# Layer 2's selective scan: the drive of eight states scaled on a turned du and turned back by TensorE

## The reference

```python
x_dbl = jnp.einsum('bkdl,kcd->bkcl', xs, x_proj_w)
dts_r, Bs, Cs = (x_dbl[:, :, :R], x_dbl[:, :, R:R + N], x_dbl[:, :, R + N:])
dts = jnp.einsum('bkrl,kdr->bkdl', dts_r, dt_proj_w)
dt = jax.nn.softplus(dts + dt_proj_b[None, :, :, None])
...
def step(h, inp):
    dt_l, u_l, B_l, C_l = inp
    dA = jnp.exp(dt_l[..., None] * A)
    h = h * dA + (dt_l * u_l)[..., None] * B_l[:, :, None, :]
    y = jnp.einsum('bkdn,bkn->bkd', h, C_l)
    return (h, y)
...
ys = ys + Ds.reshape(1, K, d, 1) * xs
```

## Time and profile before

| | before |
|---|---|
| median of three runs | 42401.93 us |
| profiled execution, its own time | 42416.64 us |
| its span, first to last instruction | 42414.8 us |
| mean granted clock of TensorE in it | 0.866 of full speed |
| busy over the span: DVE, POOL, PE, ACT | 82%, 73%, 71%, 48% |

### The profile page before, as it was taken

The page is one execution under the profiler, slowest core; times in us unless marked ns, Lnnn a source line. Parts: engine busy times, 40 slices in busy tenths (PEclk is TensorE's granted clock), DMA queues, the critical chain, the costliest instruction groups (busy, mean ns, idle before and its releaser), DMA issues. The chain is left out here.

```text
span 42414.8 us, 275743 instructions
## 1 busy us (share of the span) xinstructions
PE 30144.3 (71%) x63524; PEld 11806.2 (28%) x63524; DVE 34737.8 (82%) x35406; ACT 20384.3 (48%) x37797; POOL 31168.8 (73%) x14520
## 2 busy tenths in 40 slices
PE   6767767777777777777767777777777777777777
PEld 3232232322323223232232322323223232232322
DVE  7959779597795977959779597795977959779597
ACT  4535445354453544535445354453544535445354
POOL 6939769397693976939769397693976939769397
PEclk8888888888888888888888888888888888888888
DMA  3414234142241422414234142341423414234142
GB/s 105 151 37 152 84 105 152 37 152 85 103 152 36 152 84 104 152 36 152 84 105 151 38 152 84 105 151 37 152 84 105 151 37 152 84 105 151 37 152 84
DMA packets 1221654, 4486.01 MB, mean 106 GB/s; under 512 B 144528, under 2 KB 146072, under 8 KB 1211680
## 3 DMA queue, kind: packets, MB, share of 16 engines
q1 hardware_dynamic: 1219872, 4466.97, 30.4%
HBM read 4399.30 MB, written 67.11 MB: 105 GB/s over the span
## 5 line engine op out<-in xcount | busy, mean ns | idle before, releaser
L567 PE MATMUL PS<-WORK,CST 128*128 128x512 f32 x36096 | 20046.6, 699 | 8354.6 <-POOL WORK L483 7561.8
L472 POOL TENSOR_TENSOR WORK<-WORK,XN 128x1024 f32<-128x1024 f32 x8192 | 19246.1, 2381 | 1.3
L567 PEld LDWEIGHTS PS<-WORK,CST 128*128 128x128 f32 x36096 | 7593.5, 222 | 20499.9 <-POOL WORK L483 10379.6
L921 ACT ACTIVATE PS<-WORK,AN 128x512 f32<-128x512 f32 x16384 | 10604.8, 678 | 1806.7 <-DVE WORK L1446 1092.8
L1438 DVE TENSOR_TENSOR_SCAN PS<-PS,HST,WORK 128x512 f32<-128x512 f32 x8960 | 10972.5, 1271 | 45.5 <-ACT PS L921 32.1
L1438 DVE TENSOR_TENSOR_SCAN WORK<-PS,HST,WORK 128x512 f32<-128x512 f32 x5376 | 6583.7, 1267 | 0.0
L483 POOL TENSOR_TENSOR WORK<-WORK,CWIDE 128x1024 f32<-128x1024 f32 x2048 | 4859.8, 2373 | 136.2 <-issue 83.0
L530 POOL MEMSET XN<- 128x66 f32 x32 | 4.9, 153 | 5777.4 <-DVE SM L1288 5675.4
L921 ACT ACTIVATE WORK<-PS 128x512 f32<-128x512 f32 (+3 forms) x2752 | 1628.6, 598 | 5296.8 <-PE PS L567 4589.4
L1446 DVE TENSOR_TENSOR WORK<-PS,WORK 128x1024 f32<-128x1024 f32 x3072 | 3762.3, 1225 | 105.1
L921 ACT ACTIVATE HST<-PS 128x2 f32<-128x2 f32 x4480 | 748.9, 167 | 6154.6 <-DVE WORK L1446 6154.0
(11 more groups left out here) (158 smaller groups left out, 27665.1 us busy)
## 6 DMA issues: line engine op xcount, KB each, us to landing
XN<-xbc_rows SPq DMA_DIRECT2D x4096, 512.0 KB, 3.7
WORK<-xbc_rows SPq DMA_DIRECT2D x2048, 512.0 KB, 3.9
CWIDE<-xbc_rows SPq DMA_DIRECT2D x2048, 512.0 KB, 4.2
BIG<-in_spec_dram SPq DMA_DIRECT2D x32, 2048.0 KB, 14.7
X<-in_x_dram SPq DMA_DIRECT2D x16, 2048.0 KB, 8.7
xbc_rows<-WORK SPq DMA_DIRECT2D x512, 64.0 KB, 3.2
out_dram<-X SPq DMA_DIRECT2D x16, 2048.0 KB, 6.3
TAP<-in_cw_dram SPq DMA_DIRECT2D x1, 576.0 KB
```

The source lines that it names most:

```text
L472: nc.gpsimd.tensor_tensor(S.both(S.Q[u % 6]), S.both(S.DU[u // SN % 2]), S.wide(S.BW, u).unsqueeze(1).to_broadcast([P, 2, NT]), MUL).then_ ...
L567: return nc.tensor.matmul(o, w, r, start=start, stop=stop)
L921: return nc.scalar.activation(o, i, f, **k)
```

## The change

1. **Turned states.** For the eight states of `TURNED_STATES` POOL no longer makes the drive. Once per group, PE turns `DU` (eight transposes of 128 x 128, `turn_du`) and the rows of B (`turn_b`), and ACT copies both to SBUF (`copy_dut`, `copy_bt`). With positions on the partitions, the row B of a state is one value per partition, so ACT's `scale` makes the drive by four scaled copies of 256 columns into the single buffer `ST`. PE's `turn_back` (eight transposes) puts it, channels on the partitions again, into the pair of PSUM banks of the unit. The decay of such a unit goes to `Q` in SBUF, and the scan reads the drive from PSUM.
2. **Who weighs.** `POOL_STATES` grows from six to ten states; the eight turned ones are among them. DVE weighs the other six.
3. **y.** The former y (or, in the first direction, x times D) is added in PSUM by two matmuls ahead of a group's sum, and `take_y` moves from DVE to ACT as a plain copy.
4. **Softplus on both halves at once.** Six operations of 1024 columns in place of twelve of 512, in units 6 to 8; `log_small` once (unit 8), `sum_dt` once (unit 9), `make_du` at unit 10. The bias of dt is a ninth row of the `steps` matmul.
5. **Rows.** B and C come one row per DMA into six buffers each, B only for the eight states that POOL still drives.
6. **Order.** PE adds unit u - 1 where it added unit u, behind `turn_back(u + 2)`.

```diff
-POOL_STATES = (1, 4, 6, 9, 12, 14)
+POOL_STATES = (1, 2, 3, 5, 6, 8, 9, 11, 12, 14)
+TURNED_STATES = (2, 3, 5, 6, 8, 9, 11, 12)
...
 # POOL, in the loop over u
-                        if n == 8:
-                            sum_dt(g + 1, 0)
-                        if n == 11:
-                            sum_dt(g + 1, 1)
-                        if n == 12:
+                        if n == 9:
+                            sum_dt(g + 1)
+                        if n == 10:
                             make_du(g + 1)
-                    if u + 3 < S.units:
+                    if u + 3 < S.units and not S.is_turned(u + 3):
                         make_drive(u + 3)
...
 # PE
+                def turn_back(u):
+
+                    e.wait_ge(S.scaled, 4 * S.turned_by(u))
+                    if u >= 2:
+                        S.wait_pair(e, u - 2)
+                    for h in range(2):
+                        for j in range(4):
+                            r = nc.tensor.transpose(bank(S.banks(u)[h])[:, ch(j, P)], S.ST[:, ch(2 * j + h, P)], EYE)
+                    r.then_inc(S.turned_back, 1)
+
+                def sum_up(u):
+
+                    g, n = u // SN, u % SN
+                    if n == 0:
+                        if g:
+                            e.wait_ge(S.y_taken, g)
+                        for h in range(2):
+                            if g < NCH:
+                                w, r = SKIP[:, ch(h, P)], S.cols(BIG1, g)[:, h]
+                            else:
+                                w, r = EYE, S.cols(BIG2, g)[:, h]
+                            mm(S.like(bank(h), g)[:, 0], w, r, True, False)
+                    S.wait_weighed(e, u)
+                    for h in range(2):
+                        r = mm(bank(h), EYE, S.Q[u % 6][:, ch(h)], False, n == SN - 1)
+                    r.then_inc(S.summed, 1)
...
                     if g + 1 < KDIR * NCH:
-                        if n < 2:
-                            rows(g + 1, n)
-                        if n in (3, 4):
-                            steps(g + 1, n - 3)
-                    S.wait_weighed(e, u)
...
+                        if n in (1, 2):
+                            rows(g + 1, n - 1)
+                        if n == 4:
+                            turn_b(g + 1)
+                        if n in (5, 6):
+                            steps(g + 1, n - 5)
+                        if n == 12:
+                            turn_du(g + 1)
+                    if u + 2 < S.units and S.is_turned(u + 2):
+                        turn_back(u + 2)
+                    if u:
+                        sum_up(u - 1)
...
 # ACT
+                def scale(u):
+
+                    if u % SN == S.turned[0]:
+                        e.wait_ge(S.dut_copied, u // SN + 1)
+                        e.wait_ge(S.bt_copied, u // SN + 1)
+                    if S.turned_by(u) > 1:
+                        e.wait_ge(S.turned_back, S.turned_by(u) - 1)
+                    for j in range(4):
+                        col = SN * j + u % SN
+                        act(S.ST[:, ch(j, 2 * P)], S.DUT[:, ch(j, 2 * P)], ACT.Identity,
+                            scale=S.BT[u // SN % 2][:, col:col + 1]).then_inc(S.scaled, 1)
...
+                def take_y(g):
+
+                    e.wait_ge(S.summed, SN * (g + 1))
+                    act(S.cols(BIG2, g), S.like(PS[:, 0:2, :].rearrange("p d l -> p (d l)"), g), ACT.Copy)\
+                        .then_inc(S.y_taken, 1)
...
                     if u + 1 < S.units:
                         decays(u + 1)
+                    if n == 1 and g:
+                        take_y(g - 1)
+                    if u + 2 < S.units and S.is_turned(u + 2):
+                        scale(u + 2)
                     if g + 1 < KDIR * NCH:
-                        if n == 2:
+                        if n == 3:
                             split(g + 1)
-                        if 4 <= n < 10:
-                            softplus(g + 1, (n - 4) // 3, (n - 4) % 3)
+                        if n == 4:
+                            copy_bt(g + 1)
+                        if n in (6, 7, 8):
+                            softplus(g + 1, n - 6)
+                        if n == 13:
+                            copy_dut(g + 1)
...
 # DVE
-                log_small(0, 0)
-                log_small(0, 1)
+                log_small(0)
                 for u in range(S.units):
                     g, n = u // SN, u % SN
                     states(u)
                     if not S.on_pool(u):
                         weigh(u)
-                    if n == 1 and g:
-                        take_y(g - 1)
-                    if g + 1 < KDIR * NCH:
-                        if n == 7:
-                            log_small(g + 1, 0)
-                        if n == 10:
-                            log_small(g + 1, 1)
+                    if g + 1 < KDIR * NCH and n == 8:
+                        log_small(g + 1)
```

268 lines of the change are left out of this document (158 added, 110 removed).

## The result

| | before | after |
|---|---|---|
| median, four runs each on one chip | 42396.65 us | 47464.01 us (47445.04 to 47501.9) |
| ratio, 95% interval | | 1.1196 [1.1177, 1.1216], slower |
| span of the profiled execution | 42414.8 us | 47457.8 us |
| mean granted clock of TensorE | 0.866 | 0.891 |
| scan of layer 2, mean of the sixteen images | 1787.8 us | 2102.9 us |

The forecast was 47,350 us. The scan accounts for the whole difference: 16 x 315.1 = 5042 us, of 5043 in the span.

A forecast was written before the change was run, and what follows sets the result against it. POOL and DVE, both nearly full, bounded the kernel. Five links sum to 64.4 us even and 67.4 odd, 8.9 and 11.0 over; 31 rings an image and 16 images add 4935 us to 42,417: 47,350 us, range 44,600 to 49,600.

The forecast's parts named there:

- the ring: A group's closed chain of waits through all four engines: 64.4 us even (contiguous direction), 67.4 odd (strided); chance 0.55.
- link 4: ACT from `steps` to the end of softplus, units 6 to 8, strictly in order: 10.6 us.
- link 5: DVE's `log_small` of unit 8, in its in-order queue: 2.5 us.
- link 1: POOL's eleven operations from `log_small` to the end of weighing state 14: 25.6 us even, 26.1 odd.
- link 2: PE's sums of states 14 and 15 around `turn_back(2)`, then ACT's `take_y` and scaling of state 3: 7.85 us.
- link 3: PE from `turn_back(3)` to the second `steps`, without a rest: 17.8 us even, 20.3 odd.
- The engines' sums: Work per group: DVE 47.9 us, POOL 46.3, PE and ACT about 44; rival, busiest engine decides: 38,300 us, chance 0.08.
- PE sets it, not ACT: Rival in link 3: ACT's queue sets it, 12.2 us, 43,950 us in all; chance 0.16, shared with otherwise shorter links.
- one by one: Rival: transposes in `turn_back` run singly, 2.2 us for eight instead of 0.95; 49,850 us, chance 0.04.
- The low clock: Rival: PE's low clock level falls into links 2 and 3, up to 2.7 us a ring; 48,700 us, chance 0.14.
- The unknowns taken as nothing: Scans with decay in SBUF and drive in PSUM were taken at zero extra, and DMAs at nothing.
- The signs named: Profile after: DVE idle a quarter, ended by `turn_back` (states 2, 3, 5, 6) and softplus; POOL idle some 18 us.

The follow-up runs named there:

- experiment 2: Against the changed kernel, state 14 is weighed by DVE instead of POOL: 46256.2 us, 1.0907 of the kernel before.
- experiment 5: Against the changed kernel, DVE weighs state 13 twice into the same place: 47482.56 us, 1.1192 of the kernel before.
- experiment 8: Against the changed kernel, same parts reordered, seven turned states at other places, POOL weighing nine, `take_y` behind the scaled copies: 40100.19 us, 0.9455 of the kernel before.
- experiment 3: Against the changed kernel, `turn_back` of state 5 does its eight transposes twice: 47964.21 us, 1.1306 of the kernel before.
- experiment 7: Against the changed kernel, four turned states (2, 5, 8, 11) instead of eight, POOL weighing six: 44459.39 us, 1.0481 of the kernel before.
- experiment 10: Against the changed kernel, no turned states, POOL making all 16 drives and weighing six, the rest kept: 44334.51 us, 1.0454 of the kernel before.
- experiment 6: Against the changed kernel, part 3 undone, DVE adding y in unit 1 as before: 45375.33 us, 1.0698 of the kernel before.
- experiment 1: Against the changed kernel, ACT's `take_y` stands behind the scaling of state 3 instead of ahead: 46819.56 us, 1.1039 of the kernel before.
- experiment 11: Against the changed kernel, y by DVE again, seven turned states, steps placed anew: 39825.5 us, 0.9391 of the kernel before.

## Why the prediction was right

The step on which it rested, that the new waits close a ring longer than any engine's sum, held. Link by link (us), the forecast beside one even ring (`sum_dt` to `sum_dt`, 1651.51 to 1715.37) and one odd (1120.25 to 1187.88), both without the low clock in a link; links 4 and 5 reach to the start of what they release:

| link | even, forecast | even, measured | odd, forecast | odd, measured |
|---|---|---|---|---|
| 1 POOL to the weighing of 14 | 25.6 | 25.8 | 26.1 | 26.3 |
| 2 to `turn_back(3)` | 7.85 | 7.3 | 7.85 | 8.1 |
| 3 PE to the second `steps` | 17.8 | 17.6 | 20.3 | 20.2 |
| 4 ACT's softplus | 10.6 | 10.4 | 10.6 | 10.4 |
| 5 DVE's `log_small` | 2.5 | 2.7 | 2.5 | 2.7 |
| the ring | 64.4 | 63.9 | 67.4 | 67.6 |

- **The engines' sums.** DVE 47.9 forecast, 48.36 measured; POOL 46.3 and 46.65; ACT 44 and 43.65; PE 44 and 46.49. PE's is 2.5 too low: beside the ring a part of its work ran at the low level (at 1710.64 eight records of a sum took 5.01, elsewhere 3.60; at 1734.27 four took 3.51, elsewhere 1.98). That none of them decides was shown by experiments 2 and 5 from one side, and by 8, where the ring is short enough and DVE's 48.9 is the even group, from the other.
- **Link 2.** One term was mis-sized: in an odd group `take_y` writes strided and takes 1.88 us, where the contiguous 1.06 was taken (the upper end was 2.4):

```profile
1151.19 1.88 ACT L1017 ACTIVATE BIG<-PS 128x1024 f32<-128x1024 f32 x1 [4.10 <-PE PS L609]
```

  That is 0.8 over some 240 odd groups, 0.2 ms. The other terms of link 2 were each taken a little too long, and hide it in the odd sum: in the even ring the sum of 14 leads by 1.82 (1.91 in the forecast), `turn_back(2)` by 0.88 (0.95), `take_y` by 0.92 (1.06 and a handover), in all 7.3 for 7.85.
- **Link 3.** PE sets it, not ACT (ACT idles 2.85 us at its end). The eight transposes stand in 1.04 to 1.09 us, so the distance of 0.11 of the earlier trace rows held, and 0.87 for eight more was measured in experiment 3. The Trainium skill, "TensorE: Matmul & The Clock Gate", Part 4 (PE-mode transpose), gives about 275 ns for one of 128 x 128 in bf16 inside a kernel; one by one, by an estimate from that figure, eight would take 2.2 us. The recorded length of one agrees with it here, in float32 (median 273 ns in the trace after), the distance does not, and the distance is what a chain of them costs.
- **The low clock.** Forecast at nothing, with 2.7 us a ring as the upper end. It does fall into the ring, in a minority of groups: 32 of 208 even ones are 67 us long for 64, 24 of 224 odd ones 71 for 68. Its worth where it falls was right (2.8 us measured). That it would be rare was taken without a reason, and experiment 7, where it fell into link 2 of every group, shows that it need not have been.
- **The sum.** Even groups average 64.4 and odd ones 68.1 where 64.4 and 67.4 were forecast. That the even ones agree so well is partly luck: without the low clock they are 63.9, half a microsecond under the forecast, and the low clock, taken at nothing, adds that half on average. The scan grew by 315.1 us for 308, or 107 us over all images, a quarter of a per cent of the time.
- **The unknowns taken as nothing.** The scan with the decay in SBUF and the drive in PSUM is 2.45 for a pair, as the earlier trace rows have it for the other forms. Transfers of the rows of B and C ended none of the waits above.
- **The signs named.** DVE idles for 27% of the scan (564 of 2098.5 us; "a quarter"), ended by `turn_back` at states 2, 3 and 5 and, 5 us once a group, by softplus. At state 6 it was ACT's decay that ended the wait (1.15 us), not `turn_back` as forecast, and a wait of 2.62 us for the decay of state 8 was not in the forecast. POOL idles 17.2 us in the even group ("some 18") with no gap over 0.28 us from unit 9 to 14. ACT's carries end 14.6 us of it as forecast: the profile names other releasers for some of these waits, or none, but each ends 0.13 us after a carry. `turn_back(2)` starts 1.87 us after the weighing of 14 ends.
- **What was not tested.** The experiments lengthen or shorten links 1, 2 and 3. Links 4 and 5 were not edited alone; that they are on the ring rests on the waits in the trace, ACT's 2.85 us for `steps`, DVE's 4.96 for softplus and POOL's start of `sum_dt` right behind `log_small`.

Of the loss, 3,130 us go with the turned states and 1,932 with the rest (experiment 10, the low clock in it included); part 3 alone is worth 2,089 when taken out of the whole (6). These overlap and are not meant to add up.

## What to carry to other kernels

Where each engine has a queue in a fixed order, add up not only what each engine does but also the longest closed chain of waits from one round to the next; if it is longer than the busiest engine's work, only edits on the chain count, and moving work to an idle engine can lengthen it. Nearly the same instructions in another order (seven turned states for eight) turned 12% slower into 5.5% faster here (experiment 8), so price an order before giving up a split of the work. The quickest test for such a chain is to do one cheap piece of work twice, once on it and once beside it.

## What the runs showed of the hardware that was not expected

- ACT's copy of 1024 float32 columns from PSUM takes 1.02 us to a contiguous place in SBUF and 1.88 to a strided one; DVE's former `take_y` had 1.22 and 2.38.
- The low clock comes in runs of groups. In experiment 1 129 of 208 even groups were 2.8 us longer than the rest, with the same instructions; in direction 0 all six counted groups of an image were long in twelve images and none in three. The wait ahead does not decide it by its length alone: in after, PE waited 3.23 us for the weighing of 14 and did the next sum in 1.98; in experiment 1 it waited 3.23 as well and took 3.78. After the waits of 3.8 us in experiment 7 the sum was slow, at least in part, in all 432 groups. What decides was not settled.
- The mean granted clock rose with the rearranged orders, from 0.866 before and 0.891 in after to 0.925 and 0.926 (experiments 8 and 11). PE is busy for 88% and 84% of the scan there, 76% in after; in the even group of experiment 8 the granted clock is 1.00, and a group is as long as DVE's work.
